# Normalization and transposition of eight token tiles spread over three engines, with all tiles loaded ahead

## The reference

```
xn  = layernorm(x)
xz  = xn @ W_in.T;  a, z = split(xz)            # 4096 wide each
a   = a @ conv_w.T
att = (a * D * silu(z)) @ W_out.T
h   = relu(xn @ W1.T + b1);  h = relu(h @ W2.T + b2)
out = x + att + (h @ W3.T + b3)
```

## Time and profile before

| what | value |
|---|---|
| timed runs, us | 1846.08, 1953.33, 2122.7 (median 1953.33) |
| profiled execution, device time | 1847.9 us |
| its span, slowest core (core 5) | 1846.4 us |
| spans of the 8 cores | 1838.6 to 1846.4 us |
| granted TensorE clock, means of the cores | 0.992 to 0.996 |
| TensorE busy (matmul) | 1770.9 us, 96% of the span |
| VectorE busy | 902.7 us, 49% |
| ScalarE, GpSimd busy | 223.7 and 214.3 us, 12% each |
| first matmul of line 292 | 53.72 us |
| TensorE without a gap from | 68.08 us |

### The profile page before, as it was taken

One profiled execution on the slowest core, in us unless ns is written; L12 is line 12 of the kernel. 1 busy time (PEld: TensorE's weight loads), 2 busy tenths in 40 slices (PEclk: granted clock), 3 DMA queues, 4 the chain that ended last, 5 costly groups with the idle time before them and its releaser, 6 DMA issues.

```text
span 1846.4 us, 24801 instructions; the slowest of 8 cores (1838.6 to 1846.4 us)
## 1 busy us (share of the span) xinstructions
PE 1770.9 (96%) x9984; PEld 978.1 (53%) x9984; DVE 902.7 (49%) x1134; ACT 223.7 (12%) x350; POOL 214.3 (12%) x269
## 2 busy tenths in 40 slices
PE   2799999999999999999999999999999899999998
PEld 2344444444444444444444344444444788888887
DVE  6644444444444584444444743333332844475443
ACT  2111112222222200000000011111111000000000
POOL 0033320000000000000000000000000022222221
PEclk9899999999999999999999999999999999999999
DMA  9277774444448544444445822233337565785532
GB/s 298 71 237 213 219 218 137 137 131 124 125 134 274 155 125 125 126 123 134 137 137 169 264 88 98 104 110 114 114 114 250 174 204 176 259 272 163 181 116 69
DMA packets 58016, 296.34 MB, mean 161 GB/s; under 512 B 7600, under 2 KB 7600, under 8 KB 40368
## 3 DMA queue, kind: packets, MB, share of 16 engines
q1 hardware_dynamic: 28800, 159.40, 30.2%
q0 software_dynamic: 28816, 135.28, 21.3%
q10 hardware_dynamic: 288, 0.08, 0.0%
HBM read 227.62 MB, written 67.11 MB: 160 GB/s over the span
## 4 chain that ended last, share of the span: by engine, by line
PE 92%; DVE 5%; DMA 2%; issue 1%; ACT 0%; POOL 0%; DVEq 0%; SPq 0%; POOLq 0%; ACTq 0%
PE ps L292 73%; PE ps L748 19%; DVE sF L239 3%; DMA sF<-H2S 1%; DVE sST L311 1%; DMA sF<-X 1%; DVE sM L332 0%; DVE sW L239 0%; PE ps L347 0%; ACT sF L369 0%; DVE sM L813 0%; DVE sM L515 0%; DVEq L72 0%; POOL OUT L789 0%; POOL PS L789 0%
## 5 line engine op out<-in xcount | busy, mean ns | idle before, releaser
L292 PE MATMUL ps<-sF,sW 128*128 128x512 bf16 (+1 forms) x6272 | 1358.9, 379 | 17.1 <-DVE sM L459 9.0
L292 PEld LDWEIGHTS ps<-sF,sW 128*128 128x128 f16 x6272 | 612.9, 98 | 762.9 <-issue 28.3
L239 DVE TENSOR_TENSOR sW<-sW 128x1024 f16<-128x1024 f16 (+1 forms) x480 | 443.3, 954 | 168.2 <-DMA sW<-W 133.1
L748 PE MATMUL ps<-sW,sF 128*128 128x256 f16 x3584 | 397.2, 274 | 14.1 <-DVE sF L239 4.9
L748 PEld LDWEIGHTS ps<-sW,sF 128*128 128x128 bf16 x3584 | 352.1, 98 | 59.5 <-issue 17.0
L459 DVE TENSOR_TENSOR sM<-ps,sM 128x512 f32<-128x512 f32 x80 | 55.3, 691 | 340.7 <-ACT sM L454 340.7
L515 DVE TENSOR_TENSOR sM<-ps,sM 128x512 f32<-128x512 f32 (+1 forms) x160 | 110.2, 689 | 123.8 <-PE ps L292 123.7
L454 ACT ACTIVATE sM<-ps 128x512 f32<-128x512 f32 x80 | 47.8, 597 | 606.3 <-PE ps L292 606.3
L239 DVE TENSOR_TENSOR sF<-sF 128x2048 bf16<-128x2048 bf16 (+1 forms) x90 | 103.2, 1219 | 5.3 <-DMA sF<-H2S 5.3
L496 ACT ACTIVATE sM<-sM,sCN 128x512 bf16<-128x512 f32 x64 | 46.2, 722 | 232.9 <-DVE sM L515 232.8
L464 DVE TENSOR_TENSOR sM<-ps,sM 128x512 f32<-128x512 f32 x80 | 55.0, 687 | 24.1 <-PE ps L292 24.1
(11 more groups left out here) (34 smaller groups left out, 315.5 us busy)
## 6 DMA issues: line engine op xcount, KB each, us to landing
sW<-W SPq DMA_DIRECT2D x48, 1024.0 KB, 8.7
sW<-WC SPq DMA_DIRECT2D x32, 1024.0 KB, 6.8
sW<-WX SPq DMA_DIRECT2D x32, 512.0 KB, 8.0
sW<-WZ SPq DMA_DIRECT2D x32, 512.0 KB, 6.7
sW<-W SPq DMA_DIRECT2D x32, 512.0 KB, 6.8
sW<-WO SPq DMA_DIRECT2D x16, 1024.0 KB, 8.0
sF<-X SPq DMA_DIRECT2D x8, 1024.0 KB, 15.0
X1S<-sM POOLq DMA_DIRECT2D x16, 512.0 KB, 8.0
```

What stands on the lines that cost most here:

```text
L239: return line.do(lambda e: e.tensor_tensor(out, a, b, ALU.subtract if sub else ALU.add), c)
L292: return e.matmul(ps[bank][:], sW[:, c0 + k * 128:c0 + (k + 1) * 128], rhs[:, k * TH:(k + 1) * TH], start=st0, stop=last, skip_group_check ...
L748: return e.matmul(ps[bank][:, lo:lo + CW], lhs[:, k * TH + tp * 128:k * TH + (tp + 1) * 128], w[:, k * CW:(k + 1) * CW], start=start, stop ...
```

## The change

- All eight tiles are asked for at once. Tiles 6 and 7 go to the weight memory (`sW`, places 4 and 5 of the ring), behind them four groups of weights are asked for (one before); the first group's second half comes first. Groups 4 and 5 of the weights wait until tiles 6 and 7 are normalized.
- Normalization: tiles 0, 6, 7 on VectorE; tiles 2 and 4 on ScalarE (`norm_act`, with one more small VectorE instruction, `nmr_dve`, for the bias); tiles 1, 3, 5 on GpSimd.
- The copies out of PSUM are all on ScalarE but one, (7, 0). Banks 4 to 7 are used in place of 0 to 3. For tiles 4 to 7 half q=1 goes first.
- Forms 1 and 3 are made in four strips of 128 tokens each (`tile_form`, 8 pieces of 128 columns) in between. Form 4 is made by GpSimd in two halves of 2048 columns. Forms 6 and 7 are made later (`late_forms`), behind the sums of group 0 inside the loop.
- Product 2 of group 0 stands ahead of the transposes of tile 7.

```diff
         def xt(j):
-            s = j % 6
-            return f_f32(4 + s // 2, s % 2)
+            if j < 6:
+                return f_f32(4 + j // 2, j % 2)
+            return sW[:, (j - 2) * 4096:(j - 1) * 4096].bitcast(F32)
...
         def load_x(j):
-            if j >= 6:
-                sp.need(tk_norm[j - 6])
...
-        for j in range(6):
+        for j in range(NT):
             load_x(j)
-        load_ready(-1, 1)
+        load_ready(-1, 4)
...
-        EVB = [0, 1, 2, 3]
+        EVB = [4, 5, 6, 7]
...
+        def norm_act(j):
+
+            sbase = j * 32
+            act.need(tk_nmr[j], tk_x[j])
             if j >= 4:
...
+                act.need(tk_tr[j - 4])
+            tk_norm[j] = act.do(lambda e: e.activation(
+                xtm(j), xt(j), AF.Identity, bias=sST[:, sbase + 28:sbase + 29],
+                scale=sST[:, sbase + 27:sbase + 28]), c_act)
...
+        S(3)
+        rstd_act(3, tok_a[3])
+        nmr_dve(2)
+        norm_act(2)
+        norm(3, pool, c_pool)
+        transposes(2)
+        evac_tr(1, 0, act)
+        evac_tr(1, 1, act)
+        S(4)
+        rstd_act(4, tok_a[4])
+        nmr_dve(4)
+        transposes(3)
+        evac_tr(2, 0, act)
+        evac_tr(2, 1, act)
+        norm_act(4)
+        S(5)
+        rstd_act(5, tok_a[5])
+        norm(5, pool, c_pool)
...
+        norm(6, dve, c_dve)
+        transposes(5)
+        transposes(6)
+        S(7)
+        evac_tr(5, 1, act)
+        rstd_act(7, tok_a[7])
+        evac_tr(5, 0, act)
+        evac_tr(6, 1, act)
+        w_sum(0, 2)
+        w_sum(0, 5)
+        norm(7, dve, c_dve)
...
+        for i in range(2):
+            pool.need(tk_evac["21"][-1], tk_evac["11"][-1])
+            lo = i * 2048
+            t = w_op(pool, c_pool, OUT4[:, lo:lo + 2048], xn["21"][:, lo:lo + 2048],
+                     xn["11"][:, lo:lo + 2048], True)
+            form_tok.setdefault((0, 4), []).append(t)
```

More of the change, by code:

```diff
@@ L215, in load_w @@
             ci = 2 * (base // 4096)
-            toks = []
-            for a in range(2):
+            toks = [None, None]
+            for a in ((1, 0) if g == 0 else (0, 1)):
                 sp.need(*[gran[x] for x in range(g0 + a * gn // 2, g0 + (a + 1) * gn // 2)])
                 c0 = (p * 4 + 2 * a) * n
-                toks.append(sp.do(
+                toks[a] = sp.do(
                     lambda e, a=a, c0=c0, base=base, n=n, w=st["w"]:
@@ L325, in rstd_act, with norm, nmr_dve @@
                                                        AF.Exp, bias=0.0, scale=-0.5), c_act)
-        def norm_dve(j):
+        def norm(j, line, c):
+            sbase = j * 32
+            line.need(tk_rstd[j], tk_x[j])
+            if j >= 4:
+                line.need(tk_tr[j - 4])
+            tk_norm[j] = line.do(lambda e: e.tensor_scalar(
+                xtm(j), xt(j), sST[:, sbase + 24:sbase + 25], sST[:, sbase + 27:sbase + 28],
+                ALU.subtract, ALU.mult), c)
+        def nmr_dve(j):
             sbase = j * 32
             dve.need(tk_rstd[j])
-            if j >= 4:
[L331 to L334, removed]
+            tk_nmr[j] = dve.do(lambda e: e.tensor_scalar(
+                sST[:, sbase + 28:sbase + 29], sST[:, sbase + 24:sbase + 25],
+                sST[:, sbase + 27:sbase + 28], -1.0, ALU.mult, ALU.mult), c_dve)
+        def norm_act(j):
+            sbase = j * 32
+            act.need(tk_nmr[j], tk_x[j])
+            if j >= 4:
+                act.need(tk_tr[j - 4])
+            tk_norm[j] = act.do(lambda e: e.activation(
+                xtm(j), xt(j), AF.Identity, bias=sST[:, sbase + 28:sbase + 29],
+                scale=sST[:, sbase + 27:sbase + 28]), c_act)
+        tk_nmr = {}
         tk_tr = {}
@@ L340, in transposes @@
             pe.need(tk_norm[j], tk_id)
-            for q in range(2):
+            for q in ((0, 1) if j < 4 else (1, 0)):
                 b = EVB[ev_n[0] % 4]
@@ L351, in transposes, with evac_tr @@
                 ev_n[0] += 1
-                evac_tr(j, q)
             tk_tr[j] = tok
         XN = {"22": (0, 0), "11": (0, 4096), "12": (2, 0), "21": (2, 4096)}
-        def evac_tr(j, q):
+        def evac_tr(j, q, line):
             b, tok = tr_tok[(j, q)]
@@ L363, in evac_tr @@
             src = ps[b][:].bitcast(BF16).rearrange("p (k t) -> p k t", k=8)
-            if q == 1 and j % 2 == 1:
+            if line is dve:
                 dve.need(tok)
@@ L369, in evac_tr @@
                 t = act.do(lambda e: e.activation(dst, src, AF.Copy, bias=0.0, scale=1.0), c_act)
-            bank_tok[b] = t
+            bank_tok[b] = evac_of[(j, q)] = t
             tk_evac.setdefault(blk, []).append(t)
[L373 to L378, removed]
-        transposes(0)
[L380 to L386, removed]
@@ L408, in build_program, with by_tile @@
[L408 to L414, removed]
+        xn = {b: f_at(s, F16, lo, 4096) for b, (s, lo) in XN.items()}
+        OUT1, OUT3, OUT4 = f_at(3, F16, 0, 4096), f_at(1, F16, 0, 4096), f_at(1, F16, 4096, 4096)
+        def by_tile(ap, t):
+            return ap.rearrange("p (k t) -> p k t", k=8)[:, :, t * 128:(t + 1) * 128]
@@ new lines, in tile_form, with S @@
+        def tile_form(m, t):
+            out, a, b, sub = {1: (OUT1, "11", "22", False), 3: (OUT3, "12", "22", True)}[m]
+            dve.need(evac_of[(t, 0)] if m == 1 else evac_of[(t + 4, 0)], evac_of[(t + 4, 1)])
+            tok = w_op(dve, c_dve, by_tile(out, t), by_tile(xn[a], t), by_tile(xn[b], t), sub)
+            form[(0, m)], form_tok[(0, m)] = out, [tok]
+        tok_a = {}
+        def S(j):
+            tok_a[j] = stats_dve(j)
+        S(0)
+        rstd_act(0, tok_a[0])
+        S(1)
@@ new lines, in build_program @@
+        rstd_act(1, tok_a[1])
+        norm(0, dve, c_dve)
+        norm(1, pool, c_pool)
+        transposes(0)
+        S(2)
+        rstd_act(2, tok_a[2])
+        evac_tr(0, 0, act)
+        evac_tr(0, 1, act)
+        transposes(1)
+        S(3)
[10 more added lines that the diff above has]
+        transposes(3)
@@ new lines, in build_program @@
+        evac_tr(2, 0, act)
[4 more added lines that the diff above has]
+        norm(5, pool, c_pool)
+        evac_tr(3, 0, act)
+        evac_tr(3, 1, act)
+        transposes(4)
+        S(6)
+        rstd_act(6, tok_a[6])
+        evac_tr(4, 1, act)
+        evac_tr(4, 0, act)
+        norm(6, dve, c_dve)
[5 more added lines that the diff above has]
+        evac_tr(5, 0, act)
@@ new lines, in build_program @@
+        evac_tr(6, 1, act)
+        w_sum(0, 2)
+        w_sum(0, 5)
+        norm(7, dve, c_dve)
+        gran[8] = gran[9] = tk_norm[6]
+        gran[10] = gran[11] = tk_norm[7]
+        load_ready(-1, 5)
+        tile_form(1, 0)
+        for si in range(3):
+            form[(si, 2)], form_tok[(si, 2)] = xn["11"], [tk_evac["11"][-1]]
+        product((0, 2), 0, 2, 1, 0, [])
+        transposes(7)
+        evac_tr(6, 0, act)
+        evac_tr(7, 1, act)
+        tile_form(3, 0)
+        tile_form(1, 1)
@@ new lines, in build_program @@
+        tile_form(3, 1)
+        w_sum(0, 1)
+        evac_tr(7, 0, dve)
+        tile_form(1, 2)
+        tile_form(1, 3)
+        tile_form(3, 2)
+        tile_form(3, 3)
+        for si in range(3):
+            form[(si, 5)], form_tok[(si, 5)] = xn["22"], [tk_evac["22"][-1]]
+        for i in range(2):
[4 more added lines that the diff above has]
+            form_tok.setdefault((0, 4), []).append(t)
@@ L417, in build_program, with late_forms @@
+        form[(0, 4)] = OUT4
+        def late_forms():
+            f_sum(0, 6, xn["12"], xn["12"], xn["11"], False, F16, 2, 4096,
+                  [form_tok[(0, 3)][-1], tk_evac["12"][-1]])
+            f_sum(0, 7, xn["21"], xn["21"], xn["22"], False, F16, 2, 4096, [form_tok[(0, 4)][-1]])
+            for si in (1, 2):
+                for m in (1, 3, 4, 6, 7):
+                    form[(si, m)], form_tok[(si, m)] = form[(0, m)], form_tok[(0, m)]
         tk_bs = {}
@@ L577, in phase_a @@
             product((g, 5), si, 5, a, g, [tk_c22.get(g - 2)])
-            product((g, 2), si, 2, b, g, [tk_c11.get(g - 2), tk_s2.get(g - 2)])
+            if g > 0:
+                product((g, 2), si, 2, b, g, [tk_c11.get(g - 2), tk_s2.get(g - 2)])
             product((g, 1), si, 1, c, g, [tk_e.get(g - 2)])
@@ L608, in build_program @@
             s_next = si + 1
+            if g == 1:
+                pe.need(*[bank_tok[x] for x in EVB])
             phase_a(g)
```

21 lines of the change are left out of this document (4 added, 17 removed).

## The result

| | kernel before | changed kernel |
|---|---|---|
| timed runs | 1846.01, 1846.08, 1953.33, 2122.7, 2136.73 | 1832.91, 1833.06, 1833.62, 1834.08, 1834.56 |
| profiled execution | 1847.9 | 1833.06 |
| its span, slowest core | 1846.4 | 1831.5 |
| mean span of the 8 cores | 1843.2 | 1830.3 |

The forecast was 1834.6 us; the median is 1833.62. The ratio to the kernel before is 0.9933, 95% interval 0.9911 to 0.9954: faster, by less than 2%.

What follows compares the result with a forecast made beforehand. VectorE's work ahead of the late make_d, leaving TensorE idle at the start, was taken as the bound. Product 4 ending at 59.2 instead of 71.5 us gives 12.3, clock 1.0: 1847.9 - 13.3 = 1834.6 us, range 1826 to 1844.

Steps and rivals of the forecast that it cites:

- The bound: Start, up to group 0's product 4: gain is 71.5 us less the time it ends in the changed kernel.
- Faster by over 2%: Whole kernel below 1811 us: needs product 4 of group 0 to end at 34.5 us; chance 0.02.
- the layout's own second case: Between form 4's halves GpSimd retakes the port at once: VectorE held to 55.4, product 4 ends 61.8, gain 9.7 us.
- GpSimd normalizing 2048 columns ... I take 4.6.: Normalization of a tile on GpSimd: bounded by 1.28 and 4.5 us, taken as 4.6 from GpSimd's addition row.
- The rival of the long normalization: GpSimd's three normalizations, above 8 us each, follow each other and decide from 10.9; 15 gives 1860 us; chance 0.06.
- GpSimd's first half of form 4 needs that copy.: Form 4 on GpSimd waits for copy (7, 0), done at 46.1 us; its first half runs 46.2 to 50.8.
- If it keeps the port.: VectorE runs two strips and two sums between form 4's halves: make_d ends 54.3, product 4 59.2, gain 12.3 us.
- The hold itself: Shared port: VectorE's strips, weight sums, normalizations meeting GpSimd wait until it is done; statistics, copies and make_d are free.
- The new wait: VectorE before nmr_dve(4): tile 4's Exp comes at 26.9 us, so statistics 5 start at 27.2 instead of 25.1.
- The clock: TensorE's low clock after its idle time lost 2.1 us at the start; 1.0 of it counted as gain.
- The loads: Tiles and weights at the start all arrive ahead of their use, so the loads cost nothing.
- The rival of ScalarE's tables: ScalarE at the start reloads tables or is slower, up to 5.1 us: gain 8, 1840 us; chance 0.11.

Runs made afterwards that it cites:

- the best version: Changed kernel with tile 5 normalized and form 4 made by VectorE, plus four changes of order; 1822.71 us, ratio 0.9872, against 1834.18 for the changed kernel beside it.
- run 5: Changed kernel with other GpSimd operations for tiles 1, 3, 5: two operations with written numbers 7.21 us, one with a per-partition scalar 5.44, copy 1.89; no total given.
- run 1: Changed kernel with tile 5 normalized by VectorE instead of GpSimd; median 1830.05 us, ratio 0.9908 to the kernel before.
- run 2: Changed kernel with form 4 made by VectorE right behind make_d of group 0, instead of by GpSimd; median 1828.04 us, ratio 0.9899 to the kernel before.
- run 4: Changed kernel with all of GpSimd's start arithmetic (tiles 1, 3, 5 and form 4) on VectorE; median 1828.78 us, ratio 0.9902 to the kernel before.
- run 3: Changed kernel with tile 5 normalized by VectorE and form 4 made by VectorE behind make_d; median 1827.04 us, ratio 0.9892 to the kernel before.
- run 8: Changed kernel with 10 unused filler matmuls on TensorE between product 2 of group 0 and tile 7's transposes; median 1834.81 us, ratio 0.9949 to the kernel before.
- run 6: Kernel before with only the new loads (eight tiles at once, four weight groups behind); mean span of cores 0 to 3 1845.8 us against 1845.0.
- run 7: Kernel before with only forms 6 and 7 made late, behind group 0's weight sums; mean span of cores 0 to 3 1840.5 us against 1845.0.
- run 9: The best version: run 3 with four changes of order on ScalarE and VectorE, against the changed kernel; median 1822.71 us, ratio 0.9872 to the kernel before.

## Why the prediction was right, and where it was wrong

The steps that failed are those on GpSimd's share of the start: what its normalization costs (4.6 us taken, 7.24 measured), when it makes form 4, and who is held beside it. The total came out near the forecast all the same, and that was luck.

*The bound* held. The gain is the time by which VectorE comes earlier through its list up to `make_d`, plus a term of the clock. "Faster by over 2%" was out of reach; even the best version has 1.3%.

*The total* was near (13.3 forecast, 12.2 at mark B, 12.8 in the mean span) because four errors nearly cancel. As an estimate with the layout's own lengths, put right one after the other: GpSimd takes its turn again at once between the halves of form 4, 2.6 us less gain (the layout's own second case); its normalization takes 7.24 us, 2.6 us less; form 4 is made earlier and beside other instructions, 3.5 us more; the clock, 1.1 us more. That makes 12.7 us. The layout put right so far has the end of `make_d` at 57.5 us; measured is 57.32 + 0.68 = 58.0.

*"GpSimd normalizing 2048 columns ... I take 4.6."* It is 7.24 us, above the upper end of the bounds. The nearest row was the wrong kind: same engine and width, another form of instruction, and run 5 shows that the form is what costs. The estimate of 1.7 us worked out from the Trainium skill (GPSIMD Engine Reference, Engine selection: one input roughly at line rate) is further off; only the plain copy, 1.89 us, comes near it. With two inputs in 16 bit GpSimd takes 4.5 us for 2048 columns and VectorE 1.2, so GpSimd is almost four times slower, where that section has about twice. Its advice to keep elementwise work on VectorE is borne out by runs 1 and 2, but not for tiles 1 and 3, where run 4 loses 1.0 us. The rival of the long normalization had the direction right: the three would follow each other from 8 us on and decide from 10.9, and 7.24 stays just below that.

*"GpSimd's first half of form 4 needs that copy."* It doesn't. Form 4 is 21-11, the two blocks of tiles 0 to 3; copy (7, 0) goes to block 12. The program's own wait names blocks 21 and 11, and I read it past. So form 4 ran right behind the normalization of tile 5 (39.14 to 48.62), product 4 never waited for it, and the price fell on the two weight sums (6.26 us instead of 1.3), not on the strips at 46 us.

*"If it keeps the port."* It didn't. Between the two halves of form 4 only the first of the two waiting sums went through; the second stood until the second half was done. The layout's second case, 9.7 us, had this right and was not the one taken.

*The hold itself* was right in kind: held instructions end about one instruction's length behind GpSimd's (40.25 against 39.17, 49.17 against 48.62), and statistics take their usual 2.45 us beside it. Runs 1 to 3 take GpSimd's work away piece by piece, and A comes 4.3, 5.2 and 6.6 us earlier. That the start loses time beside GpSimd is shown, not argued.

*The new wait* of VectorE before `nmr_dve(4)` came as laid out: 2.63 us against 2.1. In the best version, with the order on ScalarE turned, 0.8 us are left.

*The clock* was mis-sized: 1.0 us of gain was counted, 2.1 us came. B - A is 590.1 us before, 588.0 after, and 587.9 in runs 1 to 4 and 8. Before, TensorE ran at the low level behind `make_d`, on the path (2.1 us lost by the earlier trace rows); now the low stretch lies ahead of `make_d`'s end or under it, and run 8 shows that less of it there gives only 0.1 us.

*The loads* cost and bring nothing, as said (run 6). *The rival of ScalarE's tables* is out: `Identity` (line 351) takes 2.09 us, and the start has one table load, as before.

```profile
L351 ACT ACTIVATE sM<-sF,sST 128x2048 bf16<-128x2048 f32 x2 | 4.2, 2092 | 0.0
...
L321 ACT ACT_TABLE_LOAD x1 | 1.3, 1283 | 12.0 <-DVE sST L315 12.0
```

Forms 6 and 7 made late give 4.4 us at A when they are taken alone (run 7), and the loads nothing (run 6). The other 5.7 of the 10.1 us belong to the rest (normalizations on ScalarE and GpSimd, forms in strips, copies on ScalarE, less GpSimd's holds); what each of these brings was not separated.

## What to carry to other kernels

Work that is given to GpSimd beside a busy VectorE can be paid for twice, once by whoever waits for it and once by VectorE's own instructions that meet it: here sums of two tensors in SBUF (`tensor_tensor`) and the normalization (`tensor_scalar`, 32 bit to 16) stood still, statistics and `make_d` did not. Give GpSimd what ends before such instructions begin (tiles 1 and 3: 1.0 us gained), and not what lies beside them (tile 5 and form 4: 6.6 us lost). Before sharing work out, move what nobody needs yet behind the one instruction that the bound engine waits for: one such move gave 4.4 us, and the four changes of order in run 9 about 5.

## What the runs showed of the hardware that was not expected

- GpSimd, 2048 columns of 32 bit to 16: copy 1.89 us; `tensor_scalar` with one operation 5.44, with two 7.21, whether the scalars stand in the instruction or in memory (7.24). Two tensors in 16 bit: 4.5 us, as in 32 bit.
- GpSimd is slowed too: the first half of form 4 began at 39.14 while VectorE's normalization still ran (to 40.25) and took 5.02 us; the second half took 4.49, and in run 1, where no such instruction ran at its start, the two took 9.05 together:

```profile
39.14 5.02 POOL L239 TENSOR_TENSOR sF<-sF 128x2048 f16<-128x2048 f16 x1
```

- Between two GpSimd instructions in a row exactly one waiting VectorE instruction got through: the first of the two weight sums (42.91, 1.80 us) released product 2 at 44.85, the second stood until 49.17.
